# Second attention: VectorE's side work moved from the ends of even steps to the ends of odd ones

## The reference

```
x = x + attention_a(norm(x))        # 16 heads of 8, normalised q and k
x = x + experts(norm(x))            # top 2 of 8 experts, 384 slots each
x = x + attention_b(norm(x))        # 16 heads of 64, position bias
x = x + experts(norm(x))

attention_b: scores = q k^T / 8 + bias[head, key - query]
             out = softmax(scores) v, then times Wo
experts:     logits = norm(x) w_router; the two largest of softmax(logits);
             each choice takes the next free slot of its expert, up to 384
```

## Time and profile before

| | |
|---|---|
| median of 3 runs | 1425.36 us (1425.13 to 1426.77) |
| the profiled execution | 1422.84 us, its span 1421.1 us |
| mean granted TensorE clock | 0.947 of full speed |
| second attention | about 446 to 1308 us of the span |
| one lap (from residual to residual) | 104.62 us (902.37 to 1006.99) |
| busy over the span | PE 87%, DVE 66%, ACT 62%, POOL 36% |

### The profile page before, as it was taken

One profiled execution on the slowest core, in us unless ns is written; L12 is line 12 of the kernel. 1 busy time (PEld: TensorE's weight loads), 2 busy tenths in 40 slices (PEclk: granted clock), 3 DMA queues, 4 the chain that ended last, 5 costly groups with the idle time before them and its releaser, 6 DMA issues.

```text
span 1421.1 us, 22477 instructions
## 1 busy us (share of the span) xinstructions
PE 1240.1 (87%) x6711; PEld 633.6 (45%) x6711; DVE 933.0 (66%) x2823; ACT 876.2 (62%) x1716; POOL 512.1 (36%) x788
## 2 busy tenths in 40 slices
PE   3899999997394899999999999999999999996392
PEld 2333434432272344544544544544544544544272
DVE  5356666664112787798798798798798797794110
ACT  1899898897041776666566576577567566662041
POOL 2000232234373233234334434434433434434255
PEclk7899999999596999999999999999999999999596
DMA  5574344448943465576576577477576565678222
GB/s 156 137 228 143 113 134 138 131 128 232 187 54 53 105 152 149 124 171 159 125 171 163 126 166 168 126 165 159 131 166 150 136 160 142 135 161 225 57 23 23
DMA packets 132937, 197.91 MB, mean 139 GB/s; under 512 B 35167, under 2 KB 76078, under 8 KB 132817
## 3 DMA queue, kind: packets, MB, share of 16 engines
q1 hardware_dynamic: 104848, 138.67, 37.9%
q0 software_dynamic: 27392, 56.76, 19.0%
q10 hardware_dynamic: 576, 1.05, 0.2%
HBM read 61.75 MB, written 39.24 MB: 71 GB/s over the span
## 4 chain that ended last, share of the span: by engine, by line
PE 69%; DVE 10%; issue 7%; DMA 5%; ACT 4%; POOL 3%; SPq 1%; DVEq 0%; POOLq 0%; ACTq 0%
PE s_ps L1461 13%; PE o_ps L922 8%; PE o_psb L1481 8%; PE o_psb L1486 7%; PE score_ps L908 6%; PE m_ps L1452 4%; PE m_ps L1435 4%; PE r_ps L1495 4%; DVE tile L1683 3%; PE r_ps L1452 3%; PE p_ps L1469 3%; DVE blocks L1696 2%; ACT probs_a L629 2%; PE H_f L1105 2%; PE O_f L1118 2%
## 5 line engine op out<-in xcount | busy, mean ns | idle before, releaser
L1597 ACT ACTIVATE tile<-tile,low 128x512 f32<-128x512 f32 x512 | 363.6, 713 | 246.9 <-DVE low L1683 245.6
L1378 POOL DMA_DIRECT2D crossed<-blocks x512 | 253.7, 506 | 488.8 <-DVE blocks L1696 443.7
L1683 DVE CUSTOM_DVE_ANT_0 tile<-s_ps,bias 128x512 f32<-128x512 f32 x512 | 330.2, 681 | 41.7 <-PE s_ps L1461 35.1
L629 ACT ACTIVATE probs_a<-score_ps,gbound 128x1024 f32<-128x1024 f32 x256 | 272.2, 1115 | 51.4 <-PE score_ps L908 51.1
L1461 PE MATMUL s_ps<-kT,qT 64*128 64x512 f32 x1024 | 265.6, 626 | 23.5 <-DVE low L1683 21.8
L1696 DVE STREAM_TRANSPOSE blocks<-tile 128x512 f32<-128x512 f32 x384 | 256.6, 693 | 0.0
L1481 PE MATMUL o_psb<-crossed,v_b 128*64 128x512 f32 x512 | 237.2, 607 | 8.3 <-DMA crossed<-blocks 8.0
L339 POOL DMA_INDIRECT slots<-rows_r,slot_r x128 | 128.5, 1004 | 69.5 <-issue 50.4
L1461 PEld LDWEIGHTS s_ps<-kT,qT 64*128 64x128 f32 x1024 | 85.3, 186 | 138.7 <-issue 80.8
L908 PE MATMUL score_ps<-q_stack,k_stack 32*128 32x512 f32 x512 | 122.8, 501 | 17.8 <-DMA q_stack<-q_parts 13.4
L922 PE MATMUL o_ps<-probs_a,v_ext 128*32 128x512 f32 x1024 | 136.2, 604 | 1.5 <-DVE o_sb L742 1.3
(11 more groups left out here) (157 smaller groups left out, 1619.2 us busy)
## 6 DMA issues: line engine op xcount, KB each, us to landing
crossed<-blocks SPq DMA_DIRECT2D x512, 96.0 KB
crossed<-blocks POOLq DMA_DIRECT2D x512, 96.0 KB
inv_row<-inv_rows SPq DMA_DIRECT2D x128, 128.0 KB, 4.2
q_parts<-parts SPq DMA_DIRECT2D x32, 256.0 KB, 3.8
k_stack<-k_parts SPq DMA_DIRECT2D x32, 256.0 KB, 4.2
q_stack<-q_parts SPq DMA_DIRECT2D x32, 256.0 KB, 4.9
w_f<-in_w SPq DMA_DIRECT2D x32, 256.0 KB, 6.0
k_parts<-parts SPq DMA_DIRECT2D x28, 256.0 KB, 3.5
```

The source lines that it names most:

```text
L629: nc.scalar.activation(probs[q % 2][:, c % 4 // 2, pair:pair + 2, :].rearrange("p h t -> p (h t)"), score_ps[c % 2][:, :], ACT.Exp, bias=g ...
L1378: pool.dma_start(strip_to(n, a, m), strip_from(n, a, m)).then_inc(crossed_sw[n % 2], 16)
L1597: nc.scalar.activation(tile[(b * NS + k) % RING][s][:, :], tile[(b * NS + k) % RING][s][:, :], ACT.Exp, bias=low[n % 2][:, s, i:i + 1], sc ...
L1683: nc.vector.tensor_tensor_reduce(out=tile[(b * NS + k) % RING][s][:, :], in0=s_ps[k % 2][s][:, :], in1=bias[:, h, off:off + S], scale=1.0, ...
```

## The change

It moves VectorE's side work between step ends, and moves the later parts of the routing:

| work | step of the lap before | after |
|---|---|---|
| `whole` for the batch after next | 4 (of the next lap) | 19, ahead of the residual |
| norm statistics and moments, next batch | 8 | 7 |
| norm rows, next batch | 10 | 9 |
| first choice of experts | 10 | 11 |
| second choice | 12 | 13 |
| run counts and gate weights | 12 | 14 |
| counts product on TensorE | 13 | 15 |
| `take_counts` | 13 | 15 |
| addresses | 14 | 16 |
| scatter pieces on POOL, behind the crossings of | steps 14, 16, 18, 4 (2, 2, 2, 2) | steps 16, 18, 4 (2, 3, 3) |

The routing's statistics (step 4), rows (6), transposes and their copy (7), logits and shift (9) and exponentials (10) stay. Two waits follow the moved counts: the counts product waits for the next batch's first k copy, and the k projection of pair 1, no longer that of pair 0, waits for `take_counts`.

```diff
-                     exps=26, first=26, second=28, runs=28, counts=(29, 1), take=29, address=30)
-        R_STEPS = range(20, 31)
-        PIECES = [range(2 * n, 2 * n + 2) for n in range(4)]
+                     exps=26, first=27, second=29, runs=30, counts=(31, 1), take=31, address=32)
+        R_STEPS = range(20, 33)
+        PIECES = [range(0, 2), range(2, 5), range(5, 8)]
...
                     if b >= 2 and n == 1:
-                        r.scatter(pool, b - 2, PIECES[3])
+                        r.scatter(pool, b - 2, PIECES[2])
                         r.landed(pool, b - 2)
...
-                    if before and more and n >= 6:
-                        r.scatter(pool, b - 1, PIECES[n - 6])
+                    if before and more and n == PAIRS - 1:
+                        r.scatter(pool, b - 1, PIECES[0])
                 if more:
                     cross(b + 1, 0)
                     if before:
-                        r.scatter(pool, b - 1, PIECES[2])
+                        r.scatter(pool, b - 1, PIECES[1])
...
-                    if n == 0 and b >= 2:
+                    if n == 1 and b >= 2:
                         wait(pe, r.late, b - 2, r.PLACE)
...
-                    r.counts(pe, b, counts, lambda: wait(pe, qk_ready, b + 1, 16) if b + 1 < B else None)
+                    r.counts(pe, b, counts, lambda: wait(pe, qk_ready, b + 2, 2) if b + 2 < B else None)
...
                 for e, d in at:
+                    if d == 3 and e + 1 < B:
+                        whole(e + 1)
+                for e, d in at:
                     if d == LAST - 1:
                         residual(e)
-                    if d == 4 and e + 1 < B:
-                        whole(e + 1)
-                    if more and d == 8:
+                    if more and d == 7:
                         norm_stats(b + 1)
                         norm_moments(b + 1)
-                    if more and d == 10:
+                    if more and d == 9:
                         norm_rows(b + 1)
```

## The result

The changed kernel took 1441.07 us (median of 4 runs, 1437.09 to 1443.91) beside 1425.53 (1425.13 to 1426.77) for the kernel before: a ratio of 1.0114, 95% interval 1.0096 to 1.0132. Run again beside other kernels it took 1442.56 against 1423.72 there, 1.0144 (1.0121 to 1.0167). So it is slower by 15 to 19 us, where 12 were forecast (1437, range 1428 to 1445).

What follows compares the result with a forecast made beforehand. Bound: TensorE's loop with VectorE's odd step, the crossing's loop close behind. Six laps at 1.66 (10.0), lap 0 at 0.8 and the last at 1.0 gave 11.8 on the median 1425.36: 1437, range 1428 to 1445.

Steps and rivals of the forecast that it cites:

- Side work in front of an even step's transposes takes a us from the crossing per us: End of odd steps on VectorE: each us there delays the transposes and takes a us from the crossing's loop.
- The crossing's duration and slack: Last transposes to TensorE's value products: duration C 10.0 to 10.43; slack 0.6 to 1.0 us plain, about 0.1 at step 8.
- Norm statistics, wait of 1.39 at step 10: Moved from step 8 to 7, they delay step 8's transposes by 1.48; TensorE waits 1.39 us (1.0 to 1.48).
- Norm rows, no wait at step 12: Moved from step 10 to 9: VectorE waits some 0.4 for POOL; TensorE doesn't wait, with 0.2 us to spare.
- The punctual `finish`, gain 0.13: Step 11's `finish` is no longer late behind the first choice; step 11's scores hide most, gain 0.13 us.
- first choice, wait of 0.4 at step 14: Moved from step 10 to 11, it delays step 12's transposes by 1.33; TensorE waits 0.4 us (0 to 0.5).
- Counts, zero: Minus 0.46 at step 13, plus 0.46 at 15; taking, addresses, run counts, weights within 1.98 idle or the longer double step.
- The last lap, 1.0 forecast: First and second choice precede transposes whose crossings TensorE already awaits: 1.3 at step 12, 1.0 at 14; the later decides, 1.0.
- Transfers hidden: Rival: the crossing is quicker when it starts later, C below 9.0; only gains stay, 1424.6 us; chance 0.11.
- Slow clock in each lap: Rival: each new crossing wait drops TensorE's clock to half, 2.8 us in each of seven laps, about 1456; chance 0.03.
- Scatter as the bound: Rival: third piece's landing takes routing's power past step 7's `finish`, some 1.5 us in six laps, about 1446; chance 0.05.
- Faster outright: Rival: late `finish` in steps 11 and 13 costs 0.66 and 0.58 in full, C short too: 1418; chance 0.04.

Runs made afterwards that it cites:

- 0.85 us more at step 5: Kernel before with eleven small VectorE instructions instead of seven at the end of step 5: 1437.73 us, ratio 1.0108; with seven 1431.58 us, 1.0056.
- the same seven instructions: Kernel before with seven small statistics instructions added on VectorE at the end of step 16: 1424.41 us, ratio 1.0008; at step 5 1431.58 us, 1.0056.
- a shorter crossing: Both kernels with each crossing transfer cut by a quarter: changed 1421.10 us, before 1419.00 us.
- the copy put ahead: Changed kernel with step 7's copy of the turned rows ahead of the norm statistics: 1445.98 us, ratio 1.0121 to the kernel before.
- the two norm kernels: Kernel before with only the norm moved (statistics to step 7, rows to 9): 1435.99 us, 1.0062; with only statistics and moments moved: 1434.88 us, 1.0058.
- the routing's half: Changed kernel with the norm back at steps 8 and 10, so only the routing moved: 1433.44 us, ratio 1.0051 to the kernel before.
- the one choice at 13: Changed kernel with the norm back at 8 and 10 and first choice at 10, second choice still at 13: 1428.95 us, ratio 1.0023 to the kernel before.
- the even-step kernel: Changed kernel with norm back at 8 and 10, choices at 10 and 12, later routing and scatter kept: 1422.78 us, ratio 0.9994 to the kernel before.

## Why the prediction was right

**Side work in front of an even step's transposes takes a us from the crossing per us.** Shown: 1.5 us of statistics moved step 8's last transposes by 1.5, and 0.85 us more at step 5 made the lap 0.9 longer, while the same seven instructions behind the transposes cost nothing that the times show, and a shorter crossing took the loss away.

**The crossing's duration and slack.** C was put at 10.0 to 10.43 and 10.34 for step 8; waits in the changed kernel give 10.45 at step 8 and 10.11 at step 12 (965.10 to 975.21). The bytes in the queues and the time from the last byte to TensorE were enough to find a slack of 0.1 us where the trace of before has no wait at all; by the 10.45 there was none.

**Norm statistics, wait of 1.39 at step 10.** TensorE waited 1.05 and came 0.39 late already, together 1.44. The prediction had the first and not the second. It gave the copy's place at step 7 but not the k projection that queues behind it; because the crossing decides, that cost nothing by itself, as the copy put ahead shows. With the 0.39 ahead of it, the double step to step 11's `finish` is 13.24 for the 13.5 forecast. The waits at step 10 of the other laps are 0.7 to 1.1 in laps 0 to 5 and 0.2 in lap 6, where TensorE had already waited 0.49 at step 8; 1.0 to 1.5 were given as the sign.

**Norm rows, no wait at step 12.** Right in batch 4's lap (0.2 in laps 3 and 6), and 0.3 us between the median laps of the two norm kernels. The forecast wait of `norm_rows` for POOL didn't come: POOL's power ends at 946.25, and VectorE, itself 0.4 late, starts the rows at 946.39.

**The punctual `finish`, gain 0.13; first choice, wait of 0.4 at step 14.** The double step to the `finish` of step 13 is 12.12 after 12.17; the wait is 0.34, and it goes when the first choice goes back. **Counts, zero:** the double step to step 17's `finish` is 0.24 longer instead of 0.46, and the one before it 0.71 (0.55 by the prediction's own figures, 972.89 less 960.19 beside 12.15). The wait isn't what closes that one. The value products allowed a `finish` at 979.00, but VectorE, with the second choice at step 13 and the run counts and gate weights at 14, comes to it at 979.13 without idle time: "stay within the 1.98" failed there. With short crossings and no wait it is 12.86 all the same, and the next one is 12.56 instead of 12.97: the price of the wait comes out there.

**A lap: 1.66 forecast.** Measured 1.75 in batch 4's lap, 1.92 in laps 2 and 5. Lap 0: 0.8 forecast, 0.87 measured. The six laps together: 10.0 forecast, 11.2 in the first profile, 14.2 in the second. That the first comes so near is in part luck: the kernel before happened to lose 1.9 in lap 1 of its profile.

**What was too small.** The sum had no term for late transfers. In lap 3 POOL's half of step 12's crossing is issued 3.1 us after SP's, in both kernels at the same place; POOL's timeline of the changed kernel, where SP had begun at 857.28:

```profile
860.35 3.91 POOL L1378 DMA_DIRECT2D crossed<-blocks  x8 [11.45 <-issue]
```

Before, TensorE waited 0.86 for it, since the rest went into the slack; now it waits 2.30. Lap 3 grew by 3.1 instead of 1.7 to 1.9, and lap 6, where POOL issues its half of step 14's crossing 2.9 us after SP (1194.04 and 1191.16) and TensorE waits 0.69 for it, by 2.6. Why POOL issues late there the profile doesn't say.

**The last lap, 1.0 forecast.** It grew by nothing in one profile, by 1.8 in the other, and by 4.9 in the routing's half. Most of the 4.9 isn't the change. The norm kernels do in the last lap what the kernel before does, and yet theirs is 2.9 and 3.2 longer, most or all of it in the last double step. The kernel before, and the one with the norm moved:

```profile
1299.10:1307.90 8.80, 8.80 (x71) 7.28 (x70) 0.69 (x1) 0.00 (x0) 5.77 (x6) 1.00 0.94 263
1310.32:1322.41 12.09, 10.91 (x71) 7.30 (x70) 0.69 (x2) 0.00 (x0) 6.28 (x7) 1.00 0.96 271
```

The same 71 products at the same clock of 1.00 take 3.3 us more, in part as idle time for which the profile shows no cause. This double step lasts 11.5 to 13.5 in the five profiles of the halves, the copy and the one choice at 13, and 8.8 to 9.5 in the nine others, and the kernel before is slower beside those five (1426.73 and 1427.21) than beside the others (1423.72 to 1425.53). So last laps of the table should be compared only inside one of the two groups. Without that double step the last lap is 82.7 in the kernel before, 82.0 and 84.2 in the changed one, 84.1 in the routing's half, and 82.3 and 83.2 in the norm kernels: -0.7 to 1.5 beside the 1.0 forecast, where kernels with the same code there differ by 0.9. The clock has a part: the mean granted clock of the last lap is 0.96, and single value products run at 0.6 or at 1.08 us, as in the earlier trace rows. How much of the rest is the clock and how much the crossing stays open, and so does what makes the last double step long.

**The rivals.** Transfers hidden: fell with C. Slow clock in each lap: fell, the granted clock is 1.00 over every one of laps 0 to 6, through waits of up to 2.3 us; it has a part in the last lap only. The Trainium skill (TensorE: Matmul & The Clock Gate, Part 1: The HAM clock gate) describes the clock as halved when TensorE has been idle and full again after sustained work. The trace agrees in kind: after the waits at the end a product took 1.04 to 1.08 us, and later ones 0.59 again. But the length of the last wait alone doesn't decide: 2.35 us in the last lap left 1.04, while 2.30 in lap 3 of the same profile and 2.95 in that of the routing's half left 0.61. Scatter as the bound: fell, the even-step kernel has it. Faster outright: fell.

## What to carry to other kernels

An engine's idle time before its next wait isn't free everywhere: ask what each of its outputs releases, and put side work behind the output with the longest journey, here the transposes with 10 us of transfers, not in front of it. A path that shows no wait may still be full; add up issue, bytes and landing against the consumer's start to find its slack, and spend none of it where late transfers happen by chance. Before mending one of two waits in a row, see which of them sets the consumer's start.

## What was not expected of the hardware

A crossing of 1.57 MB in 16 transfers, issued on two queues, takes 10.0 to 10.5 us from the start of the last transposes to the consumer where both halves are issued on time, 1.4 of them after its last bytes, and a quarter fewer bytes left three waits in the changed kernel's eight laps. POOL's issue was 3.1 us late at one place in the program in both kernels, without anything that the profile shows it to wait for. The same 71 matrix products of the last double step took 8.8 us in some profiles and 12.1 in another, at a granted clock of 1.00 in both.
